# A gated-delta attention layer on one NeuronCore: VectorE's order inside a slot, with the 16-wide triangular inverse in other places and the second half of the decays one slot later

## The reference

```python
mixed = silu(causal_conv4(x @ w_qkv));  q, k, v = split(mixed)      # 16 key heads, 32 value heads of 128
beta  = sigmoid(x @ w_b);  g = -(exp(A_log) * softplus(x @ w_a + dt_bias))
q, k  = l2norm(q) / sqrt(128), l2norm(k)
def step(state, (q_t, k_t, v_t, g_t, b_t)):                          # 1024 tokens, one after the other
    state  = state * exp(g_t)
    delta  = (v_t - k_t @ state) * b_t
    state  = state + outer(k_t, delta)
    out_t  = q_t @ state
core = norm_w * rmsnorm(outs) * silu(x @ w_z)
x    = x + core @ w_out
```

## Time and profile before

| what | value |
|---|---|
| time, median of 3 | 4167.84 us (4165.18 to 4172.16) |
| the profiled execution | 4168.05 us, its span 4166.1 us |
| TensorE busy | 3997.3 us, 96% |
| VectorE busy | 3196.9 us, 77% |
| ScalarE busy | 2592.6 us, 62% |
| GpSimd busy | 958.8 us, 23% |
| granted TensorE clock, mean | 0.991 of full speed |

### The profile page before, as it was taken

How to read it: one execution, slowest core, us unless ns; L and a number is a source line. 1 busy time by engine, 2 the same in 40 slices (tenths; PEclk the granted TensorE clock), 3 DMA queues, 4 the chain that set the end, 5 groups by cost and what they waited for, 6 DMA issues and landing times. The chain is left out here.

```text
span 4166.1 us, 83038 instructions
## 1 busy us (share of the span) xinstructions
PE 3997.3 (96%) x29437; PEld 2282.0 (55%) x29437; DVE 3196.9 (77%) x8334; ACT 2592.6 (62%) x6087; POOL 958.8 (23%) x1110
## 2 busy tenths in 40 slices
PE   7999999999999999999999999998899999999999
PEld 4555556556555555566565555555444444444444
DVE  4777887787787777877778877777447989898940
ACT  3566676666666666666666666666445656574643
POOL 1224333234333243333333333332100000000000
PEclk9999999999999999999999999999999999999999
DMA  3223334333433433343334333334304545454510
GB/s 131 83 72 84 87 86 90 85 80 85 92 77 85 120 82 85 90 86 85 81 87 92 75 87 85 82 80 97 83 1 132 164 148 168 147 175 153 183 57 10
DMA packets 290733, 402.99 MB, mean 97 GB/s; under 512 B 25774, under 2 KB 125362, under 8 KB 290258
## 3 DMA queue, kind: packets, MB, share of 16 engines
q1 hardware_dynamic: 253458, 330.57, 26.1%
q0 software_dynamic: 36864, 67.13, 12.0%
HBM read 288.56 MB, written 113.25 MB: 96 GB/s over the span
## 5 line engine op out<-in xcount | busy, mean ns | idle before, releaser
L676 PE MATMUL bank<-x_blocks,rows_b 128*128 128x512 f32 x1536 | 713.0, 597 | 0.9 <-ACT partial L914 0.9
L1306 DVE SCALAR_TENSOR_TENSOR conv<-raw,conv_w,conv 128x1024 f32<-128x1024 f32 x384 | 522.7, 1361 | 61.9 <-ACT conv L1008 56.8
L676 PE MATMUL bank<-x_blocks,w_pair 128*128 128x512 f32 x1152 | 549.9, 605 | 14.8 <-DVE x_blocks L1277 4.5
L831 PE MATMUL bank<-w_out_unit,oT 128*128 128x512 f32 x1008 | 491.4, 610 | 0.9 <-ACT out_stage L931 0.9
L676 PEld LDWEIGHTS bank<-x_blocks,rows_b 128*128 128x128 f32 x1536 | 274.9, 190 | 249.1 <-issue 231.3
L1662 PE MATMUL bank<-xnT_f,w_gu 128*128 128x512 f32 x704 | 324.5, 605 | 1.2 <-ACT xnT_f L2161 0.9
L1291 DVE SCALAR_TENSOR_TENSOR oT<-bank,norm_w,z 128x256 f32<-128x256 f32 x252 | 119.2, 473 | 261.4 <-PE bank L761 260.3
L676 PEld LDWEIGHTS bank<-x_blocks,w_pair 128*128 128x128 f32 x1152 | 206.8, 193 | 205.5 <-issue 169.5
L2231 ACT ACTIVATE step_decay<-dt,rate 128x512 f32<-128x512 f32 x256 | 183.4, 720 | 217.1 <-DVE h L2340 215.0
L1681 PE MATMUL bank<-w_down,hidden 128*128 128x512 f32 x704 | 316.9, 594 | 1.7 <-DVE x_blocks L1740 1.7
L1671 PE MATMUL bank<-xnT_f,w_gu 128*128 128x512 f32 x704 | 316.8, 593 | 0.5 <-DVE hidden L1702 0.5
(11 more groups left out here) (270 smaller groups left out, 8360.8 us busy)
## 6 DMA issues: line engine op xcount, KB each, us to landing
x_after<-out_stage POOLq DMA_DIRECT2D x256, 256.0 KB, 4.2
rows_b<-bc_rows SPq DMA_DIRECT2D x256, 256.0 KB, 3.6
rows_c<-bc_rows SPq DMA_DIRECT2D x256, 256.0 KB, 3.7
w_pair<-in_w_qkv SPq DMA_DIRECT2D x128, 256.0 KB, 3.9
decay<-gc_rows SPq DMA_DIRECT2D x64, 512.0 KB, 5.0
z<-z_rows SPq DMA_DIRECT2D x64, 512.0 KB, 5.1
z_rows<-x_blocks SPq DMA_DIRECT2D x96, 256.0 KB, 5.8
w_pair<-in_w_z SPq DMA_DIRECT2D x64, 256.0 KB, 3.3
```

Of the source, the lines that this page charges most:

```text
L676: made = e.matmul(bank[:, :], weight[:, j, :], part(0, m)[:, j, :], start=j == 0 and m in (1, 5), stop=j == 1, skip_group_check=True)
L831: made = e.matmul(out_rows(N, t)[:, :], turned_to(N, t)[:, r, :], w_out[:, N % 2, r, :], start=r == 0, stop=r == REP - 1)
L1306: e.scalar_tensor_tensor(acc, raw[:, i, tap:tap + T], conv_w[:, tap, col:col + 1], acc, ALU.mult, ALU.add).then_inc(on["conv"], 1)
```

## The change

It moves work of VectorE between places of the loop and changes two slot numbers; no operation is added or dropped. `base_inverse` now has five sections: 1 holds steps j = 1 to 3, 2 holds 4 to 6, 3 holds 7 to 10, 4 holds 11 to 14 and the identity. Sections 0, 1 and 4 stand between `resid` and the read of product a and gated o, in places 2, 3 and 4 for half 0 and in places 6, 7 and 0 for half 1. Sections 2 and 3 stand behind the two convolution taps and ahead of the read of product b and `state`, in places 3 and 7. Nothing of `base_inverse` is left at the end of a slot. The second half of the decays is subtracted in place 2 rather than 1, and GpSimd's select of it moves with it.

```diff
@@ -1178,7 +1178,7 @@
                     e.tensor_tensor(even, even, odd, ALU.add).then_inc(on["base"], 1)
                 done = step + 8
                 for j in range(1, BASE - 1):
-                    if section == (1 if j < 7 else 2 if j < 11 else 3):
+                    if section == (1 if j < 4 else 2 if j < 7 else 3 if j < 11 else 4):
                         lanes = [16 * (lane // 16) + j for lane in range(32)]
                         row, cols = odd[:, :, 0:j], n_base[:, :, 0:j]
                         col = even[:, :, j:j + 1].broadcast_to([P, NC, j])
@@ -1189,7 +1189,7 @@
                         e.wait_ge(on["base"], done + 2)
                         e.tensor_tensor(cols, cols, row, ALU.add).then_inc(on["base"], 1)
                     done += 3
-                if section == 3:
+                if section == 4:
                     e.wait_ge(on["base"], done)
                     e.tensor_tensor(n_base[:, :, :], n_base[:, :, :], wide(c["base_ident"]), ALU.add).then_inc(
                         on["base"], 1)
@@ -1351,7 +1351,7 @@
                     if n is not None:
                         evict_pair(n, a, 0)
                 for a in range(2):
-                    n = unit_at_only(slot, 8 + a)
+                    n = unit_at_only(slot, 8 + 2 * a)
                     if n is not None:
                         N = n
                         if a == 0:
@@ -1374,16 +1374,19 @@
                     if n is not None:
                         e.wait_ge(on["mask"], 2 * n + a + 1)
                         turn_base()
+                for a in range(2):
+                    for section, at in ((0, 10), (1, 11), (4, 12)):
+                        n = unit_at_only(slot, at + 4 * a)
+                        if n is not None:
+                            base_inverse(n, a, section)
                 read_at(slot, "a")
                 gate_out(slot)
-                n = unit_at_only(slot, 10)
-                if n is not None:
-                    base_inverse(n, 0, 0)
                 convolve(slot, (2, 1))
                 for a in range(2):
                     n = unit_at_only(slot, 11 + 4 * a)
                     if n is not None:
-                        base_inverse(n, a, 1)
+                        base_inverse(n, a, 2)
+                        base_inverse(n, a, 3)
 
                 read_at(slot, "b")
 
@@ -1430,15 +1433,7 @@
                         if n >= 1:
                             e.wait_ge(on["u_pe"], 8 * (n - 1) + HALF * a + HALF)
                         turn_inverse(a)
-                    n = unit_at_only(slot, 10 + 4 * a)
-                    if n is not None and a == 1:
-                        base_inverse(n, a, 0)
-                    n = unit_at_only(slot, 11 + 4 * a)
-                    if n is not None:
-                        base_inverse(n, a, 2)
-                    n = unit_at_only(slot, 12 + 4 * a)
-                    if n is not None:
-                        base_inverse(n, a, 3)
+
         def gpsimd(e):
             c["make"](e)
             e.memset(raw[:, :, 0:PAD], 0.0).then_inc(on["zeroed"], 1)
```

## The result

The changed kernel takes 4334.31 us in the median (4333.81 to 4343.44, 5 runs) against 4165.18 us (4162.54 to 4172.16, 5 runs) of the kernel before, measured with it: 1.041 times as long, 95% interval 1.0395 to 1.0426. The sign was forecast, the size was not: 4248 was said and at most 4292, so 169 us were lost where 81 were expected.

A forecast was written before the change was run, and what follows sets the result against it. TensorE, busy 977 of 1000 us, was taken as the bound. Per unit 1.45 us (places 7 and 0) plus 1.3 (place 2), 31 times, made 85 us, less 4 at the ends: 4248 us, range 4195 to 4292.

The forecast's parts named there:

- The gain at `resid`: Places 1 and 5: `resid` in time, but TensorE meets ScalarE's `off` at L608; 0.47 of 1.03 us kept, nothing in place 5.
- Places 7 and 0: Moved steps make `state` late for L712: 1.92 us taken; less place 1's 0.47, 1.45 per unit, bounds 0.69 and 2.21.
- the stall only changes its victim: Place 0: GpSimd's select slows step 11 to 14 operations instead of the taps, so nothing is won back: 1.92 us.
- the case of 2.68: Place 0: GpSimd's mask, starting just ahead of the taps, also stalls them, making `state` 2.68 us late.
- Place 2: Decays and section 0 delay the read of product a, so L617 waits for `off`: 1.3 us per unit, 1.0 to 1.8.
- Places 3, 4, 5 and 6: No loss in 3, 4 and 6, where later `state` or taps have room; no gain in 5, L608 already at ScalarE's copy.
- the next place to tip: Place 4: `state` about 0.3 us later, 1.1 with a stall by the mask, against 1.3 of room; no loss.
- The ends: First and last units, with longer `resid` waits up to 4.2 us: a gain of 4 us credited once.
- single wait: Rival: only one of the new waits, in place 0 or place 2, comes true; 4209 or 4204 to 4225; chance 0.12.
- a gain: Rival: the gain at `resid` is kept and neither new wait appears; 4149, or 4115 with all kept; chance 0.10.
- both new waits: L712 waiting for `state` in place 0 and L617 for ScalarE's `off` in place 2, over 1 us each per unit.
- what was to show it: `resid` gone; waits at L712, L617 and L608; ScalarE's wait before L1008 about 3.6 us; unit period some 2.7 us longer.

The follow-up runs named there:

- e7: Changed kernel, with GpSimd's mask of half 1 waiting until `state` of place 0 is written: 4312.18 us, 1.0355 of before.
- e12: Changed kernel, with GpSimd's sums of weights in place 2 waiting until section 0 of that half is done: 4299.28 us, 1.0308 of before.
- e5: Changed kernel, with ScalarE's first-level copy `off` moved ahead of the Silu of z: 4289.47 us, 1.03 of before.
- e6: Kernel before, with ScalarE's first-level copy `off` moved ahead of the Silu of z: 4158.12 us, 0.998 of before.
- e9: Kernel before, with the edits of e8 and e6 together: 4109.39 us, 0.9862 of before.
- e8: Kernel before, with its base inverse spread over VectorE's idle time, decays and place 2 as before: 4155.93 us, 0.9979 of before.
- e11: Changed kernel, with place 2's read of product a ahead of section 0 and half 1's steps 11 to 14 ending place 0 again: 4178.43 us, 1.0035.
- e4: Changed kernel, with steps 7 to 10 of half 1 behind `o` at the end of place 7 again: 4351.12 us, 1.0439 of before.

## Why the prediction had the sign and missed the size

The order's own effects were worked out rightly in both places. What failed is the price of the stalls beside GpSimd: the sum held one of 0.76 us in place 0 and none in place 2, and the runs showed 0.87 (by a row) and 0.84 (e7) in place 0 and 1.30 (e12) in place 2.

**The gain at `resid`: right.** The step said that L608 runs into ScalarE's copy and that 0.47 us of place 1 and nothing of place 5 is kept. Place 1 kept 0.45; place 5 lost 0.10. That the copy is what swallows it is shown by e5 and by the pair e6 and e9: the same edit on ScalarE gives 9 us where `resid` is late (e6), and 45 (e5) and 47 (e9 against e8) where it is not.

**Places 7 and 0: the mechanism right, the term too small.** The step offered 1.16, 1.92 or 2.68 us for zero, one or two stalls, and took 1.92 with the words that "the stall only changes its victim". It was 2.93. Both stalls come: the select on step 11 (L1188 1.12 instead of 0.25 us, read from the row; no run moves the select alone), the mask on the taps (0.84 us, shown by e7). The step that failed is the choice of 1.92: the text had itself put the mask just ahead of the taps, which is the case of 2.68, and gave no reason against it. The 0.25 above 2.68 stands in the rows. Stalls of 0.87 and 0.83 in place of two of 0.76 make 0.18; and VectorE reaches `col_beta` 11.35 us behind place 7's L712 (1380.08), where the forecast's 1404.08 is 11.28 behind that of before (1392.80), which is 0.07 more.

**Place 2: the order right, the stall missed.** The forecast was 1.3 us, with 1.8 as the bound. Without the sums of weights beside it, place 2 takes 13.06, 1.38 over before: that is the order's own price, as worked out. The other 1.30 is the stall of two operations. The step that failed is the stall: the sum put it at nothing, and the bound at one of 0.49, the excess of the one long execution of L1170 that the trace before held. The rows after show stalls that last until 0.1 to 0.2 us behind the end of the other instruction. GpSimd's timeline of the kernel before has two sums of weights in place 2, just where section 0 was to go (from 1427.5 on by the forecast):

```profile
1426.90 1.02 POOL L1460 TENSOR_TENSOR rows_b<-w_pair 128x256 f32<-128x256 f32 x1
...
1428.14 0.73 POOL L1460 TENSOR_TENSOR rows_b<-w_pair,rows_b 128x256 f32<-128x256 f32 x1 [0.22 <-PE bank L676]
```

I had not put that timeline beside the new places of the moved operations.

**Places 3, 4, 5 and 6: right in the main.** I said nothing for all, and place 4 "the next place to tip": it tipped by 0.10, with the taps at 3.78 us beside the mask and a sum of weights. Place 5 is 0.10 longer too: ScalarE's read of product a (L917) starts 2.99 us behind L712 instead of 2.90, and the copy `off` behind it 10.06 instead of 9.96.

**The sum.** Per unit 2.75 was forecast and 5.37 measured. The difference of 2.62 is 1.01 in places 7 and 0, 1.38 in place 2, 0.20 in places 4 and 5 and 0.02 in place 1. Of it 0.84 (e7) and 1.30 (e12) are stalls beside GpSimd that the sum did not hold. The ends gave nothing back either: I credited 4 us, and e11 is 13 us slower than before at an equal unit.

**The rivals.** Neither single wait nor a gain came; both new waits did. Of what was to show it, the waits at L712, L617 and L608 are there, and the period grew by 5.4 rather than 2.7 us. L712 waits 0.8 us rather than over 1, since L831, which was not on the list, has waited 1.32 for `oT` just ahead of it. ScalarE's wait before L1008 is 4.94 us where 3.6 was said.

What stays open: which moved operation makes the ends of e11 longer, and what lowers the granted clock in e4.

## What to carry to other kernels

Idle time of an engine is worth filling only up to the moment at which the next instruction behind it is due. Here the time ahead of the gated o was idle, but the reads and the state behind it were not: ask of every operation that is put in front of something who waits for that something, in each place of the loop by itself.

When work is moved on VectorE, lay GpSimd's timeline beside its new place. In the rows of the changed kernel, a VectorE operation with two operands in SBUF that met a running sum of weights, mask or select of GpSimd was mostly 0.4 to 1.2 us longer (0.27 at least, a last tap beside the end of a sum). The subtraction of the decays (L1371), beside a GpSimd operation that started after it, took its 1.23 us. Waits put on GpSimd alone gave 22 and 35 us back.

A wait that is the only one in the list can hide another just behind it. Removing `resid` alone gave 10 us and moving ScalarE's copy alone gave 9, both together 58.

## What the runs showed of the hardware that was not expected

Very short VectorE operations were held up beside GpSimd for as long as long ones: L1170, 0.29 us alone, took 1.20 us beside a sum of weights of 1.02 us, and L1188, 0.25 us alone, took 1.12 us beside a select of 1.09 us, while the two taps lost 0.83 us.

The Trainium skill ("SBUF — State Buffer", section "SBUF: two separate sides") says that of a VectorE instruction with two inputs in SBUF and a GpSimd instruction that reads SBUF, the one that starts first keeps the shared port pair for its whole length, and the other is blocked. L1188 agrees: the select started 0.07 us ahead of it (1393.07 and 1393.14). L1170 does not settle the order: the sum is stamped 0.02 us behind it (1419.11 and 1419.09), and it was L1170 that was held up. The transposes with one operand, in the same place beside the select, took 1.83 us for four as before.
